# Softplus minimum folded into VectorE's last step, and one convolution step moved into the long run of the others (Mamba block and FFN on one Trainium2 core)

## The reference

```python
xi, z = split(x @ W_in.T)                        # 512 channels each
u  = silu(causal_conv(xi, conv_w, 4 taps) + conv_b)
dbl = u @ W_xproj.T                              # 16 for dt, 16 B, 16 C
dt = softplus(dbl[..., :16] @ W_dt.T + b_dt)     # the step that is changed
dA = exp(dt * A);  h = h * dA + (dt * u) * B     # scan over the tokens, 16 states per channel
y  = (sum_s h * C + u * D_skip) * silu(z)
x  = layernorm(x + y @ W_out.T)
x  = layernorm(x + (silu(x @ wg.T) * (x @ wu.T)) @ wd.T)
```

## Time and profile before

| | us |
|---|---|
| median of 3 runs (lowest, highest) | 1805.21 (1802.66, 1806.15) |
| the profiled execution | 1806.15 |
| its span in the trace | 1804.4 |
| busy in the span: PE, ACT, DVE, POOL | 1738.6, 1713.0, 1703.1, 1494.9 |

### The profile page before, as it was taken

One profiled execution on the slowest core, in us unless ns is written; L12 is line 12 of the kernel. 1 busy time (PEld: TensorE's weight loads), 2 busy tenths in 40 slices (PEclk: granted clock), 3 DMA queues, 4 the chain that ended last, 5 costly groups with the idle time before them and its releaser, 6 DMA issues.

```text
span 1804.4 us, 40427 instructions
## 1 busy us (share of the span) xinstructions
PE 1738.6 (96%) x15678; PEld 1213.7 (67%) x15678; DVE 1703.1 (94%) x2003; ACT 1713.0 (95%) x2907; POOL 1494.9 (83%) x852
## 2 busy tenths in 40 slices
PE   7779999999999999999999999999999999999997
PEld 3456676767667676676767767676676767667676
DVE  5989999999999999999999999999999999999974
ACT  6899999999999999999999999999999999999971
POOL 5887997979979797997979979797997979989850
PEclk9899999999999999999999999999999999999999
DMA  7040120303013040221303013040221304012000
GB/s 210 1 120 1 10 112 15 118 1 97 36 15 118 14 118 1 31 102 15 118 2 105 28 15 118 15 118 1 46 87 15 118 1 119 15 37 84 1 25 24
DMA packets 171487, 100.57 MB, mean 56 GB/s; under 512 B 139408, under 2 KB 157584, under 8 KB 163232
## 3 DMA queue, kind: packets, MB, share of 16 engines
q1 hardware_dynamic: 171296, 97.98, 19.2%
HBM read 88.52 MB, written 9.44 MB: 54 GB/s over the span
## 4 chain that ended last, share of the span: by engine, by line
PE 45%; ACT 26%; DVE 15%; issue 9%; POOL 4%; DMA 0%; ACTq 0%; POOLq 0%; DVEq 0%
PE ring L1174 17%; PE tp L1153 13%; ACT decay L704 9%; DVE h L915 8%; ACT hT L711 7%; PE yb L1167 7%; PE ring L1266 4%; DVE acc L936 4%; POOL drive L568 3%; PE ring L1211 2%; ACT L741 2%; ACT acc L720 1%; PE ring L1232 1%; ACT sz L741 1%; ACT u L737 1%
## 5 line engine op out<-in xcount | busy, mean ns | idle before, releaser
L568 POOL TENSOR_TENSOR drive<-dtu,b_all 128x1024 f32<-128x1024 f32 x511 | 1215.5, 2413 | 7.9 <-DVE h L915 5.6
L704 ACT ACTIVATE decay<-dt,a_neg 128x512 f32<-128x512 f32 x1024 | 706.6, 718 | 9.4 <-DVE h L915 8.6
L1153 PEld LDWEIGHTS tp<-ident,h 128*128 128x128 f32 x4096 | 463.2, 141 | 245.8 <-issue 122.6
L915 DVE TENSOR_TENSOR_SCAN h<-decay,h,drive 128x512 f32<-128x512 f32 x512 | 620.6, 1268 | 7.5 <-ACT decay L704 2.6
L915 DVE TENSOR_TENSOR_SCAN h<-decay,drive 128x512 f32<-128x512 f32 x512 | 592.7, 1210 | 26.0 <-ACT decay L704 23.8
L711 ACT ACTIVATE hT<-tp 128x512 f32<-128x512 f32 x1024 | 595.9, 618 | 15.8 <-PE tp L1153 14.9
L1153 PE MATMUL tp<-ident,h 128*128 128x128 f32 x4096 | 564.0, 277 | 40.2 <-ACT hT L711 31.5
L1167 PE MATMUL yb<-hT,diag_c 128*32 128x128 f32 x8192 | 276.2, 277 | 6.4 <-ACT yt L732 5.3
L1167 PEld LDWEIGHTS yb<-hT,diag_c 128*32 128x32 f32 x8192 | 211.1, 110 | 82.2 <-issue 48.3
L1174 PE MATMUL ring<-xt,w_in 128*128 128x512 f32 x512 | 245.1, 602 | 2.4 <-ACT acc L752 2.4
L936 DVE SCALAR_TENSOR_TENSOR acc<-xi,cw,acc 128x512 f32<-128x512 f32 x189 | 160.3, 869 | 14.6 <-ACT xi L722 10.7
(11 more groups left out here) (134 smaller groups left out, 1673.5 us busy)
## 6 DMA issues: line engine op xcount, KB each, us to landing
b_all<-bc_scratch SPq DMA_DIRECT2D x63, 1024.0 KB, 7.3
xt<-in_xT SPq DMA_DIRECT2D x16, 512.0 KB, 4.6
res<-in_x SPq DMA_DIRECT2D x16, 512.0 KB, 6.2
out<-res SPq DMA_DIRECT2D x15, 512.0 KB, 2.9
c_col<-bc_scratch SPq DMA_DIRECT2D x256, 2.0 KB, 2.4
bc_scratch<-dbl SPq DMA_DIRECT2D x16, 64.0 KB, 1.6
b_all<-bc_scratch SPq DMA_DIRECT2D x2, 512.0 KB, 4.5
w_g<-in_w_gT SPq DMA_DIRECT2D x1, 768.0 KB, 7.3
```

Of the source, the lines that this page charges most:

```text
L568: tt(drive[:, j % 4, :, :], src, b_all[:, n:n + 2, :], ALU.mult).then_inc(g_dr, 1)
L704: act(decay[decay_slot(k.parity, i)][:, :], dt[:, cb, :], ACT.Exp, scale=a_neg[:, cb, n:n + 1]).then_inc(a_da, 1)
L915: nc.vector.tensor_tensor_scan(h[:, h_slot(k.parity, q), at:at + T, i % 4], decay[decay_slot(k.parity, i)][:, :], drive[:, (i // 2) % 4, i ...
L1153: last = nc.tensor.transpose(tp[g % 2][:, b * P:(b + 1) * P], h[:, h_slot(k.parity, q), t0:t0 + TS, :].rearrange("p t s -> p (t s)"), iden ...
```

## The change

VectorE no longer clamps. ScalarE's Exp reads `acc` and writes `dt`; in place of waiting for VectorE it waits for its own bias step. The last step of softplus becomes one `scalar_tensor_tensor`, max(min(., 40), x). All 31 clamps of 128 x 1024 and the two of 128 x 512 at the start go away, as do two semaphores. In the steady list, the convolution step at (3, 3) moves to (5, 3), ahead of the other eleven; in the first chunk it stays at (3, 2).

```diff
 DVE_SIDE = {
-    (2, 1): [("skip", 3), ("clamp", 1)], (3, 3): [("conv", 0, 0), ("r1", 0)], (4, 2): [("r1", 1)],
-    (5, 3): [("max", 1), ("norm", 0), ("conv", 0, 1), ("conv", 1, 0), ...
+    (2, 1): [("skip", 3)], (3, 3): [("r1", 0)], (4, 2): [("r1", 1)],
+    (5, 3): [("max", 1), ("norm", 0), ("conv", 0, 0), ("conv", 0, 1), ("conv", 1, 0), ...
-    (14, 0): [("clamp", 0), ("r2", 0), ("skip", 2)], (14, 1): [("max", 0)], (15, 0): [("r2", 1)],
+    (14, 0): [("r2", 0), ("skip", 2)], (14, 1): [("max", 0)], (15, 0): [("r2", 1)],
...
             def softplus_log(k, half):
                 two = dt[:, 2 * half:2 * half + 2, :]
-                wait(eng, v_mn, k.count(2, half + 1))
-                act(two, two, ACT.Exp).then_inc(a_e, 1)
+                wait(eng, a_xb, k.count(4, 2 * half + 2))
+                act(two, acc[:, 2 * half:2 * half + 2, :], ACT.Exp).then_inc(a_e, 1)
...
-            def clamp(k, half):
-                two = slice(2 * half, 2 * half + 2)
-                wait(eng, a_xb, k.count(4, 2 * half + 2))
-                wait(eng, a_da, k.count(STEPS, -STEPS + 32 * (half + 1)))
-                ts(dt[:, two, :], acc[:, two, :], 40.0, None, ALU.min).then_inc(v_mn, 1)
...
             def softplus_max(k, half):
                 wait(eng, a_ln, k.count(2, half + 1))
-                tt(dt[:, two, :], acc[:, two, :], dt[:, two, :], ALU.max).then_inc(v_dt, 1)
+                stt(dt[:, two, :], dt[:, two, :], 40.0, acc[:, two, :], ALU.min, ALU.max).then_inc(v_dt, 1)
```

More of the change, by code:

```diff
@@ L84 @@
 DVE_SIDE = {
-    (2, 1): [("skip", 3), ("clamp", 1)], (3, 3): [("conv", 0, 0), ("r1", 0)], (4, 2): [("r1", 1)],
-    (5, 3): [("max", 1), ("norm", 0), ("conv", 0, 1), ("conv", 1, 0), ("conv", 1, 1), ("conv", 2, 0), ("conv", 2, 1), ("conv", 3, 0), ("conv", 3, 1)],
+    (2, 1): [("skip", 3)], (3, 3): [("r1", 0)], (4, 2): [("r1", 1)],
+    (5, 3): [("max", 1), ("norm", 0), ("conv", 0, 0), ("conv", 0, 1), ("conv", 1, 0), ("conv", 1, 1), ("conv", 2, 0), ("conv", 2, 1), ("conv", 3, 0), ("conv", 3, 1)],
     (6, 0): [("gs", 0), ("gs", 1)], (6, 2): [("hid", 0)], (7, 0): [("gs", 2)], (7, 1): [("hid", 1)],
@@ L124 @@
 DVE_FIRST = {
-    (0, -1): [("clamp", 1)], (2, 2): [("max", 1)], (3, 2): [("conv", 0, 0)],
+    (2, 2): [("max", 1)], (3, 2): [("conv", 0, 0)],
     (7, 0): [("conv", 0, 1), ("conv", 1, 0), ("conv", 1, 1), ("conv", 2, 0), ("conv", 2, 1), ("conv", 3, 0), ("conv", 3, 1)],
-    (10, 0): [("skip", 0)], (12, 3): [("skip", 1)], (13, 0): [("clamp", 0)], (13, 3): [("max", 0)],
+    (10, 0): [("skip", 0)], (12, 3): [("skip", 1)], (13, 3): [("max", 0)],
     (14, 2): [("skip", 2)],
@@ L176 @@
 DVE_LAST = {
-    (2, 1): [("skip", 3)], (2, 2): [("clamp", 1)], (3, 1): [("r1", 0)], (3, 3): [("r1", 1)],
+    (2, 1): [("skip", 3)], (3, 1): [("r1", 0)], (3, 3): [("r1", 1)],
     (4, 1): [("norm", 0)], (5, 3): [("gs", 0)], (6, 1): [("gs", 1)],
@@ L418, in mamba_ffn @@
         a_y = sem("a_y"); a_x1T = sem("a_x1T"); a_th = sem("a_th"); a_o = sem("a_o"); a_set = sem("a_set")
-        v_h = sem("v_h"); v_x1 = sem("v_x1"); v_y = sem("v_y"); v_conv = sem("v_conv"); v_mn = sem("v_mn"); v_dt = sem("v_dt")
+        v_h = sem("v_h"); v_x1 = sem("v_x1"); v_y = sem("v_y"); v_conv = sem("v_conv"); v_dt = sem("v_dt")
         v_r1 = sem("v_r1"); v_s1 = sem("v_s1"); v_gs = sem("v_gs")
@@ L430, in mamba_ffn @@
         e_n = sem("e_n"); e_var = sem("e_var"); e_std = sem("e_std"); e_o = sem("e_o")
-        f_mn = sem("f_mn"); f_e = sem("f_e"); f_ln = sem("f_ln"); f_dt = sem("f_dt"); f_dtu = sem("f_dtu"); f_diag = sem("f_diag"); f_conv = sem("f_conv"); f_b = sem("f_b"); f_dr = sem("f_dr")
+        f_e = sem("f_e"); f_ln = sem("f_ln"); f_dt = sem("f_dt"); f_dtu = sem("f_dtu"); f_diag = sem("f_diag"); f_conv = sem("f_conv"); f_b = sem("f_b"); f_dr = sem("f_dr")
         conv_loads = [
@@ L848, in _ @@
             add_bias(k0, 1)
-            for cb, (mn, e, ln) in enumerate(((f_mn, f_e, f_ln), (v_mn, a_e, a_ln))):
-                eng.wait_ge(mn, 1)
-                act(dt[:, cb, :], dt[:, cb, :], ACT.Exp).then_inc(e, 1)
+            for cb, (e, ln) in enumerate(((f_e, f_ln), (a_e, a_ln))):
+                eng.wait_ge(a_xb, cb + 1)
+                act(dt[:, cb, :], acc[:, cb, :], ACT.Exp).then_inc(e, 1)
                 eng.wait_ge(e, 1)
@@ L999, in item @@
                 i, *part = of or [None]
[L1000 to L1004, removed]
                 if what == "max":
@@ L1044, in _ @@
             ts(a_neg[:, :, :], a_neg[:, :, :], -1.0, None, ALU.mult).then_inc(v_set, 1)
-            for cb, done in enumerate((f_mn, v_mn)):
-                eng.wait_ge(a_xb, cb + 1)
-                ts(dt[:, cb, :], acc[:, cb, :], 40.0, None, ALU.min).then_inc(done, 1)
             for cb, (ln, done) in enumerate(((f_ln, f_dt), (a_ln, v_dt))):
                 eng.wait_ge(ln, 1)
-                tt(dt[:, cb, :], acc[:, cb, :], dt[:, cb, :], ALU.max).then_inc(done, 1)
+                stt(dt[:, cb, :], dt[:, cb, :], 40.0, acc[:, cb, :], ALU.min, ALU.max).then_inc(done, 1)
                 if cb == 0:
```

## The result

The kernel after takes 1809.41 us in the median of 14 runs (1807.82 to 1812.77), the kernel before 1805.19 (1802.66 to 1808.91, 14 runs). The ratio is 1.0026, with an interval of 1.0019 to 1.0032. The profiled execution of after took 1807.82 us with a span of 1806.1, its fastest of the 14. So the two traces differ by only 1.7 us in span, less than the medians (4.2), and the difference has to be read piece by piece.

A forecast was written before the change was run, and what follows sets the result against it. ScalarE and TensorE, the fullest engines, bound the kernel, with VectorE's long run arriving just in time. Seven pairs +7.2, start -0.35, last chunk -0.3 give +6.6 us on 1805.21: 1811.8 us, range 1802.5 to 1815.5.

The forecast's parts named there:

- no change: Rival: idle time of TensorE and ScalarE absorbs the 0.74 us, only small gains stay, 1802.9 us; chance 0.18.
- The run does not start earlier against decay 23, and VectorE only waits more: Ahead of the long run: VectorE's 2.7 us saved go into waiting for ScalarE; idle time 4.9 to about 11 us a pair.
- The 0.19 us wait of the odd chunk goes, the one of 0.63 us stays: ScalarE's decay waits for VectorE: the one at 594.38 disappears, the one at 676.31 stays because Ln gates max.
- Gain of the clamps and the lone step, 0.24 us a pair: Steady chunks, work ahead of ScalarE's wait: 0.19 us gained in an odd chunk, 0.05 allowed in an even one.
- Form of the last step, 0: Softplus's last step with a constant costs no more than before: 0 taken, upper bound 3.6 us in all.
- Loss of 0.70 in the odd and 0.57 us in the even chunk: Behind the run of twelve: hid 0 and heads come 0.74 us later, and TensorE and ScalarE shift together.
- The pair, +1.03: Two steady chunks: 0.24 us gained, 1.27 lost, so +1.03 us; seven pairs give +7.2 us.
- The start, -0.35 of 0 to 0.85 us: First chunk: ScalarE's first wide Exp no longer waits 0.85 us for the clamp; 0.35 us of it taken as gain.
- The last chunk, -0.3: Last chunk loses one clamp: a gain of 0 to 0.8 us, 0.3 taken.
- The moved step takes the short price: In the long run the twelfth step costs 0.74 us, not 1.91 us as alone, since GpSimd stands idle.
- The rule on shared interfaces: GpSimd and VectorE contend for SBUF interfaces; by this rule the change removes both kinds of collision and speaks for a gain.
- the case "faster": Rival: freed VectorE time and undisturbed GpSimd remove both ScalarE waits, 0.82 us a pair, 1798.8 us; chance 0.12.

The follow-up runs named there:

- Experiment 6: After, with ScalarE's silu of u 2 and u 3 ahead of tanh 0: 1813.90 us; with only u 2 ahead: 1808.84 us.
- experiment 3: First kernel: clamps out, step at (3, 3) except in chunk 1, there in the run: 1802.22 us. Second: after, step alone in chunk 1 only: 1816.94 us.
- experiment 5: Clamps out, step in the run in chunk 1 only, plus GpSimd's heads of chunk 0 moved from (8, 0) to (7, 0): 1803.02 us.
- the thirteen steps: After with one more convolution step at the head of the long run, its result read by nothing: 1818.84 to 1822.23 us, ratio 1.0089.
- experiment 4: Clamps out, step alone at (3, 3), GpSimd waiting once in chunk 1 for that step ahead of drive 9: 1800.62 us, ratio 0.9977.
- experiment 1: After with the step back at (3, 3): 1804.99 us, six runs 1799.96 to 1802.90, six 1807.07 to 1812.69. Before with only the step moved: 1809.93 us.

## Why the prediction was right, point by point

It forecast 1811.8 us and slower by over 0.2%; measured were 1809.41 us and +0.23% by the medians (interval of the ratio 0.19 to 0.32%). The mechanism of the steady part is the one forecast: the run is 0.78 us longer (9.03 against 8.25), and ScalarE and TensorE wait for it. Two of its terms were too small and by luck nearly made up for each other, one wait was put to the wrong engine, and the term of the start was far too small. The range, 1802.5 to 1815.5 us, would have held "no change" as well, so the sign and the pair (217.0 forecast, 217.10 measured) say more for the forecast than the hit.

- **The run does not start earlier against decay 23, and VectorE only waits more.** Right in the sum: VectorE's idle time went from 4.90 to 10.70 us a pair (forecast about 11). Wrong in the wait: the freed time was to be "spent waiting for ScalarE", but over four chunks the waits for decays grew only from 4.6 to 8.0 us, and those for the products of TensorE that the residual steps read (L952, in before L958) from 0.8 to 8.7. Scan 23 itself idles no more than before: no bracket in the odd chunk, 0.23 us in the even one (at 708.42), where it was 0.32.
- **The 0.19 us wait of the odd chunk goes, the one of 0.63 us stays.** Right: ScalarE's decays at 589.85 and 594.93 have no bracket, and at 673.19 it still waits 0.63 us, behind the Ln that gates max.
- **Gain of the clamps and the lone step, 0.24 us a pair.** The clamps alone give 0.34, and with the step moved they give 0.00, since the kernels with and without them both have 217.10. The two edits were added up as if each kept its worth beside the other. What the clamps free lies ahead of the run, and there the lone step's removal had freed more than could be used. This reason is argued from the waits; the 0.00 is measured.
- **Form of the last step, 0.** Right: max took 1212 ns over eight instances in before and takes 1213 in after.
- **Loss of 0.70 in the odd and 0.57 us in the even chunk.** Counted from the start of the run (in before 606.96 and 715.18), tanh 0 starts 0.79 and 0.66 us later, up 0 0.53 in the odd chunk, up 1's products 0.64 and 0.47. ScalarE's figures, 0.79 + 0.66 = 1.45, are what the pair lost against the kernel with only the minimum moved (217.10 - 215.65). The forecast took those of TensorE, 1.27, and wrote that the two engines would shift together. Experiment 6 shows that to be half right: they do follow each other, but ScalarE's path is the later one by 0.5 us a pair.
- **The pair, +1.03.** Measured +1.11. Nearly the right sum, from two terms that were both too small: the move costs 1.45 where the clamps are out, and taking the clamps out gives 0.34 where the step isn't moved.
- **The start, -0.35 of 0 to 0.85 us.** This term was mis-sized. In the profiled executions the start gives back 6.2 us. Worked out from the medians, it is 4.2 - 7.45 - 0.45 = -3.7. It was priced from ScalarE's wait for a clamp alone. But the moved step is in chunk 1 too, and what stood next to it there wasn't looked at. By the traces it is worth 1.2 to 1.6 us there where it takes 2.7 us (157.01 in before), and 9.3 us where it is held for 9.34. How often the kernel before has the long hold isn't known; putting the step back into chunk 1 of after cost 3.8 us in the mean (0.4 to 7, experiment 3). The rest of the 6.2 us lies ahead of skip 3 of chunk 1. Some 3 us at that point go with the place of the clock's dip, with clamps and without (below). So the moved step explains a part of the -3.7, and how much stays open.
- **The last chunk, -0.3.** The piece behind the last steady run grew by 0.45, where half a pair's loss, 0.55, was due for the chunk that it begins with: -0.1. As small as forecast.
- **The moved step takes the short price.** Right: 9.03 us for twelve, GpSimd idle for 12.34 us. That is 1.34 us more than in before and not 0.7: GpSimd's last drive ends 3.23 us ahead of the run (599.82) where it was 2.67 (604.29).
- **The rule on shared interfaces.** It was noted that it speaks for the change, and it was priced as the case "faster", in steady chunks. There the trace gave it nothing, since there VectorE waits anyway. Where it mattered was chunk 1, where GpSimd's instructions follow one another without a gap.

So the sum of the forecast, 7.2 - 0.35 - 0.3 = +6.55, stands against 7.45 + 0.45 - 3.7 = +4.2: the steady part and the end were 1.0 us too low, the start 3.35 too high, and the difference is the error of 2.4 us.

Single runs of one kernel differ by 3 us and more, and the traces show two places where this can arise. One is the lone step in chunk 1. The other is TensorE's clock: in every trace the granted clock (a share of 2.4 GHz) dips during the first 130 us, at different places. This is the stretch behind the first maximum, in the kernel with the minimum alone moved and in the kernel of experiment 3:

```profile
120.00:130.00 10.00, 8.75 (x86) 6.29 (x90) 7.29 (x5) 7.53 (x14) 5.17 (x3) 0.64 0.64 251
```

```profile
120.00:130.00 10.00, 8.16 (x105) 6.21 (x106) 9.70 (x8) 9.99 (x20) 7.43 (x6) 1.00 0.60 226
```

A mean clock of 0.64 is 0.7 of the stretch at 1.2 instead of 2.4 GHz ((1 - 0.64)/0.5); two products of the dt projection take 2.08 us where they take 1.12 in the other, and ScalarE idles for 2.5 of the 10 us. In both TensorE had been busy for 14.5 to 14.6 of the 20 us ahead of it. The chunk 1 runs of the two kernels of experiment 6, which have no lone step, start at 173.73 and 173.74 us with 0.62 in this stretch, those of after, of the first kernel of experiment 3 and of experiment 5 at 168.96 to 170.24 with 0.99 to 1.00. Skip 3 of chunk 1 starts at 148.0 to 148.5 us in the three traces with 0.62 to 0.64, and at 143.7 to 145.6 in the seven with 0.97 to 1.00, one of which still has the clamps (145.38): some 3 us go with the dip. Two traces have 0.83 in it, that of before with 148.31 and that of the thirteen steps with 146.69. What decides where the dip falls wasn't found.

Open is also a small thing: the same steady lists give a pair of 215.57 us in experiment 4, 215.65 in the kernel with the minimum alone moved and 215.85 in experiment 3, and 217.10 or 217.30 with the run of twelve in after and behind a lone step in chunk 1. How the engines stand to one another when the steady part begins seems to be kept, by 0.1 to 0.3 us a pair. No run tells why.

## What to carry to other kernels

An instruction moved from a place where its engine has slack to a place where others wait for it costs its own length there, even if it gets shorter by the move: 1.6 to 1.9 us saved where nobody waited brought nothing, 0.75 us added where two engines waited cost 0.7. Price an edit of a shared list of work in every chunk that uses it; the first and second chunk differ in what runs beside it, and there the sign was the other one. And where VectorE reads two tiles in SBUF, look for a place at which GpSimd stands still, or make it stand still: one wait of 1.01 us on GpSimd was worth 4.5 us (ratio 0.9977 against 1.0002; by their intervals 1 to 8 us).

## What the hardware showed that was not expected

**VectorE can be held by GpSimd over many instructions.** A 128x512 step with two inputs in SBUF takes 0.72 to 0.75 us beside an idle GpSimd, 1.5 to 2.0 us at (3, 3) in the steady chunks, 2.69 and 2.73 us in two traces of chunk 1, and 9.34 and 9.35 us in two others, in both over five instructions of GpSimd that follow one another without a gap over 0.1 us. Nothing in VectorE's own rows tells them apart. Scans, which read the decay from PSUM, keep their 1.1 to 1.3 us beside the same stream. In the traces with 2.69 and 2.73 us VectorE got in at the first boundary, and GpSimd's next instruction was the one to wait: its diag_c took 1.49 us instead of 1.05.

```profile
152.12 7.03 POOL L568 TENSOR_TENSOR drive<-dtu,b_all 128x1024 f32<-128x1024 f32 x3
159.12 1.49 POOL L576 TENSOR_TENSOR diag_c<-of_token,c_col 128x512 f32<-128x512 f32 x1
```

That is from before, where the step ran from 157.01 to 159.70. The Trainium skill, "SBUF — State Buffer", on the two separate sides of SBUF, says that a VectorE operation with two SBUF inputs and a GpSimd operation that reads SBUF contend for a shared pair of ports, that whichever starts first holds it for the whole instruction, and that the other is fully blocked. The traces agree that the block is complete: in eleven of twelve the maximum of chunk 0 ends 1.1 us behind the stream, about its own length, whether it began 1.9, 2.9 or 6.0 us ahead of the stream's end. It goes further than the rule in one thing. A wait for one GpSimd instruction would be 2.4 us at most; in the trace with 9.34 us GpSimd kept the pair at four boundaries in a row, and VectorE got it only when GpSimd had to wait for VectorE. Who gets the pair at a boundary differs between these traces, though the step begins 0.2 us behind the start of a drive in all four. They are of four programs; that it varies between runs of one program as well is not shown by a trace, but is what the two groups of experiment 1 suggest.
